# A tile of the shared expert's down projection moved in between the second and third group of value products

## The reference

```python
h = concat([cls, patches @ W_lin.T + b_lin], axis=1)     # 1 + 196 rows
h = concat([h, txt], axis=1)                             # 325 rows
# attention: 12 heads of 16, RMS norm and rotary turn of q and k, causal
x = layernorm(h)
q, k, v = split(x @ qkv_w)
probs = softmax(mask(rotary(rms(q)) @ rotary(rms(k)).T * 0.12))
h = h + (probs @ v) @ c_proj_w.T
# one shared expert and three routed ones, of which two are taken per token
x = layernorm(h)
shared = (silu(x @ shared_gate) * (x @ shared_up)) @ shared_down
w = normalised top-2 of sigmoid(x @ router_w + routing_bias)
routed = sum_e w[e] * ((silu(x @ gate_e) * (x @ up_e)) @ down_e)
h = h + shared + routed
```

## Time and profile before

| | |
|---|---|
| median of 3 runs | 1613.54 us (1612.33 to 1616.0) |
| the profiled execution, its time | 1613.08 us |
| the profiled execution, its span | 1611.1 us |
| TensorE busy | 1582.6 us, 98% of the span |
| weight loads busy | 1487.5 us, 92% |
| VectorE busy | 1202.4 us, 75% |
| ScalarE busy | 879.8 us, 55% |
| GpSimd busy | 410.7 us, 25% |
| mean granted clock of TensorE | 0.994 |

### The profile page before, as it was taken

The page is one execution under the profiler, slowest core; times in us unless marked ns, Lnnn a source line. Parts: engine busy times, 40 slices in busy tenths (PEclk is TensorE's granted clock), DMA queues, the critical chain, the costliest instruction groups (busy, mean ns, idle before and its releaser), DMA issues.

```text
span 1611.1 us, 46516 instructions
## 1 busy us (share of the span) xinstructions
PE 1582.6 (98%) x16632; PEld 1487.5 (92%) x16632; DVE 1202.4 (75%) x3383; ACT 879.8 (55%) x1896; POOL 410.7 (25%) x647
## 2 busy tenths in 40 slices
PE   6899999999999999999999999999999999999999
PEld 6699999999999999999999999999999999998988
DVE  6777787777877677777778777778877777877765
ACT  4556555555545565455556555566555566555552
POOL 1332321223212323213233212233212323212320
PEclk8899999999999999999999999999999999999999
DMA  6211211112211112111111111111111111111110
GB/s 216 72 42 60 69 60 42 48 57 69 69 42 48 56 62 69 49 48 44 47 57 57 47 41 37 51 51 57 49 42 38 49 49 57 53 39 34 35 33 13
DMA packets 75382, 86.80 MB, mean 54 GB/s; under 512 B 12721, under 2 KB 64329, under 8 KB 75209
## 3 DMA queue, kind: packets, MB, share of 16 engines
q1 hardware_dynamic: 64776, 65.45, 11.9%
q10 hardware_dynamic: 10560, 20.74, 3.9%
HBM read 32.44 MB, written 12.51 MB: 28 GB/s over the span
## 4 chain that ended last, share of the span: by engine, by line
PE 91%; DMA 3%; DVE 3%; ACT 1%; issue 1%; POOL 0%; SPq 0%; DVEq 0%; POOLq 0%
PE ps L426 84%; PE ps L429 6%; DMA kt<-kt 3%; PE ps L626 2%; DVE kt L1175 1%; DVE o L1072 0%; DVE xt L1103 0%; SPq L368 0%; DMA probs<-in_x_first 0%; ACT rows L817 0%; DVE stats L1092 0%; ACT wf L810 0%; POOL rstd L1015 0%; DVE qk_split L1168 0%; DVE rotated L1163 0%
## 5 line engine op out<-in xcount | busy, mean ns | idle before, releaser
L426 PE MATMUL ps<-xt,wf 64*128 64x326 f32 x6912 | 598.5, 316 | 0.0
L426 PEld LDWEIGHTS ps<-xt,wf 64*128 64x128 f32 x6912 | 539.3, 186 | 11.2 <-ACT qt L810 7.0
L426 PE MATMUL ps<-w_down_s,ht 128*128 128x192 f32 (+1 forms) x2304 | 413.8, 329 | 0.0
L426 PEld LDWEIGHTS ps<-w_down_s,ht 128*128 128x128 f32 (+1 forms) x2304 | 351.0, 174 | 14.5 <-issue 0.2
L1049 DVE SCALAR_TENSOR_TENSOR gated<-tanh_g,ps 128x326 f32<-128x326 f32 x384 | 188.7, 491 | 131.7 <-ACT tanh_g L824 130.3
L817 ACT ACTIVATE rows<-h,rstd 128x192 f32<-128x192 f32 (+2 forms) x279 | 151.1, 564 | 212.9 <-POOL rstd L1019 208.0
L835 ACT ACTIVATE probs<-ps 128x792 f32<-128x792 f32 (+1 forms) x384 | 254.3, 663 | 19.1 <-PE ps L426 18.9
L1008 POOL TENSOR_TENSOR probs<-probs,causal 128x512 f32<-128x512 f32 x192 | 229.0, 1193 | 131.8 <-ACT probs L835 131.8
L824 ACT ACTIVATE tanh_g<-ps 128x326 f32<-128x326 f32 x384 | 170.2, 443 | 164.9 <-PE ps L426 163.0
L1002 POOL TENSOR_TENSOR probs<-probs,causal 69x140 f32<-69x140 f32 x192 | 89.3, 465 | 479.6 <-ACT probs L835 479.5
L1055 DVE TENSOR_TENSOR ht<-gated,ps 128x326 f32<-128x326 f32 x384 | 190.1, 495 | 13.1
(11 more groups left out here) (105 smaller groups left out, 2009.2 us busy)
## 6 DMA issues: line engine op xcount, KB each, us to landing
kt<-kt SPq DMA_DIRECT2D x384, 40.8 KB, 1.8
x_s<-in_xp ACTq DMA_DIRECT2D x40, 384.0 KB, 3.2
qt<-qt SPq DMA_DIRECT2D x132, 81.5 KB, 1.9
residual<-h SPq DMA_DIRECT2D x31, 288.0 KB, 2.4
out<-o SPq DMA_DIRECT2D x32, 192.0 KB
qt<-qt ACTq DMA_DIRECT2D x60, 81.5 KB, 2.0
kept_rows<-embed_rows SPq DMA_DIRECT2D x44, 96.0 KB, 1.7
h<-kept_rows SPq DMA_DIRECT2D x30, 95.2 KB
```

The costliest lines, as they stand in the source:

```text
L426: return nc.tensor.matmul(dst, lhs, rhs, start=first, stop=last)
```

## The change

The tile `down(0, 0)` is taken from its place behind `norm1_turn` and put between the second and the third value group. `norm1_turn` then follows the third group, and `y_to_rows` follows `norm1_turn` with nothing between. The wait inside `down(0, 0)`, which was for all 12 hidden chunks, is now for 11 of them in turns with attention. `norm1_turn` has a wait of its own for all 12. No other engine's program is changed.

```diff
@@ down
                 if t == 0 and e == 0:
-                    pe.wait_ge(h_ready.sem, h_ready.at(b, UNITS if A else UNITS - 2))
+                    pe.wait_ge(h_ready.sem, h_ready.at(b, UNITS - 1 if A else UNITS - 2))
@@ turn of TensorE
                 if A:
-                    for g in range(GROUPS):
+                    for g in range(GROUPS - 1):
                         value(g, b2, F)
-                if A:
+                    down(0, 0, b3)
+                    value(GROUPS - 1, b2, F)
                     if L:
                         norm1_turn(b1, F)
-                    down(0, 0, b3)
                     y_to_rows(b2)
                     down(0, 1, b3)
                     down(0, 2, b3)
```

## The result

| | before | changed |
|---|---|---|
| median of 10 runs | 1611.47 us (1610.25 to 1616.0) | 1615.85 us (1613.85 to 1618.14) |
| profiled execution, time and span | 1613.08, 1611.1 us | 1615.89, 1613.8 us |

The account below looks back on a forecast made before the run. The prediction took TensorE's own sequence to bound the kernel. Terms of +0.11 us in 30 turns and +0.68 us in the last summed to +4.0 us, so 1617.5 us, with a range of 1611.5 to 1620.5.

Parts of the forecast that it names:

- What bounds the kernel: Whole kernel: TensorE is busy 98% of the span, so a change is worth what it does to TensorE's sequence.
- mask wait gone: Before the third value group: the tile fills TensorE's wait for GpSimd's last mask, -0.23 us a turn.
- leaving the value products once more: From the second value group to the full-width tile: an added change of shape costs +0.17 us a turn.
- coming back: From the full-width tile to the third value group: the return to 32-column products costs +0.25 us a turn.
- wait for the third copy: Before the value-sum transposes: without the tile as cover, TensorE waits for ScalarE's third copy, +0.04 us a turn.
- value-sum transposes behind a wait: At the value-sum transposes: behind a wait the first loads reach their result in 1.24 us, not 1.35, -0.11 a turn.
- The sum, +0.11 a turn and +0.68 in the last: Over 30 turns with row transposes and the 31st without: +0.11 us each and +0.68 us, +4.0 us in all.
- The costs put at nothing: Around the moved tile: its hidden-chunk wait, the later row transposes and VectorE's later reciprocal are covered and cost nothing.
- Rival 2: At the return to value products: group 2's loads run ahead of the tile, -3.8 us, 1609.7 us; chance 0.12.
- Rival 1: At the return to value products: coming back costs 0.20 us or less, +2.4 us, 1615.9 us; chance 0.33.
- Rival 3: In the turns: later row transposes, the copy or leaving cost more than seen, +6.1 us, 1619.6 and above; chance 0.05.

Follow-up runs that it names:

- experiment 5: Both kernels with an extra mask-sized GpSimd multiplication ahead of the last mask; against the kernel before, 1.0207 in the old order, 1.0031 in the new.
- experiments 2: Both kernels with VectorE masking one of the last pair's two heads; against the kernel before, 0.9966 in the old order, 1.0017 in the new.
- experiment 6: The changed kernel with the shared expert's first tile ahead of all three value groups, which form one block again; 0.9997 against the kernel before.
- experiment 4: The changed kernel with the first tile between value groups 1 and 2 and the second between 2 and 3; 1.0104 against the kernel before.

## Why the prediction was right

**What bounds the kernel** held: what the stretch gained or lost came through in the time, 3.7 us by the trace and 3.4 timed for the change, 31.4 and 33 for the late mask of experiment 5.

**The terms.** The first column is the prediction's sum for one turn; the second is read from first loads, of the changed kernel, of the kernel before and of experiments 2 and 6.

| us a turn | forecast | measured |
|---|---|---|
| mask wait gone | -0.23 | -0.25 |
| leaving the value products once more | +0.17 | +0.14 |
| coming back | +0.25 | +0.25 |
| wait for the third copy | +0.04 | +0.07 |
| value-sum transposes behind a wait | -0.11 | -0.10 |
| sum | +0.12 | +0.10 (0.11 from the rounded terms) |

Coming back came out at the 1.17 us forecast from the tile's first load to group 2's, against 0.92 among full-width neighbours; the forecast had it from the opening and the last turn. Leaving costs 0.14 wherever nothing waited before: 3.17 - 3 x 1.01 in experiment 6, and 2.15 - 2 x 1.01 (0.13 by the rounded times) and 1.15 - 1.01 in the changed kernel. The forecast read its 0.17 behind group 2 of the kernel before, which had started after a wait and took 1.07 us for its loads and not 1.04; these 0.03 us belong to the mask wait, which is 0.22 up to group 2's first load (2.23 against 2.02 for two groups) and 0.25 with them. The wait for the copy was priced too low: from the row transposes to the next load it is 0.63 us, against 0.56 where nothing waits. The value-sum transposes then take 0.93 us to the next load and not 1.03. So the mechanism is as forecast, and three of its terms were each off by 0.02 to 0.03 us; that these cancel but for 0.02 is luck.

**The sum, +0.11 a turn and +0.68 in the last.** Measured 0.10 and 0.67, so 3.7 us in place of 4.0. The timed runs say 3.4 (2.1 to 4.7). That it comes out slower by more than 0.2%, as the forecast had it, is not shown: 0.21% lies on that line.

**The costs put at nothing** were nothing: the relaxed wait, the later row transposes (VectorE's second subtraction ends at 843.09, the projection's first load comes 1.55 us after), and VectorE's reciprocal, which starts on time at 843.05, 1.24 us after the first of the transposes that it waits for.

**The rivals.** Rival 2, that group 2's loads run ahead of the tile, falls: it is 1.17 or 1.18 us in every kernel in which the tile stands before value products, with 0.92 wanted, and group 2's first load and product start together (840.03) in the changed kernel. The Trainium skill, TensorE: Matmul & The Clock Gate, section Step-by-step: what each phase is for, says that loads are pulled ahead of products in flight where row groups don't conflict or the background buffer is the target. From the full-width tile to value products they are not pulled ahead in any of these runs. Rival 1, the cheap end, wanted 1.12 us there and falls by the same row as a mechanism. Its number, +0.06 us a turn, is also farther from the measured 0.10 than the forecast's +0.11; what was cheaper than forecast was leaving, not coming back. Rival 3 had nothing to show. What the runs show is that the price goes with each crossing: 0.39 us there and back for the one that the change adds (0.14 + 0.25), 0.39 again for the second in experiment 4, and 0.13 less for the one change of shape that experiment 6 saves. The Trainium skill, TensorEngine Tiling (Array Packing), section Key Properties, says that a change of tiling mode drains TensorE. The 0.23 us of idle time agree with it; no run here looks inside the engine.

## What to carry to other kernels

Before you put work of another shape into a wait, compare the way there and back with the wait: here 0.32 us against 0.22, and in experiment 5, where the wait was 1.2 us, the same move won. Take the price of a crossing from any place where the trace has one, an opening or a last turn too, before you count a hidden wait as gain. Take it from a place where nothing waits: the price of leaving was read behind a wait as 0.17 us, and is 0.14 where nothing waits. Where an idle engine can make the awaited thing come earlier, as VectorE did with half of the last mask, the wait goes without any reordering, and this was the only version here that beat both kernels.

## What the runs showed of the hardware that I had not expected

A value group that starts after a wait takes 1.07 us for its 24 loads, one that comes right behind the full-width tile 1.04. A GpSimd product of 128x512 whose two inputs are the same small table, written to a buffer that nothing reads, delayed the next one by 1.00 us (its own record is 1.04 long), where a mask of that size takes 1.19. And VectorE took 0.51 us for half of what takes GpSimd 1.19 whole, while GpSimd needed 0.73 for the other half, more than the 0.60 that half of 1.19 would be.
